# A graph network on one core: the last stage forms its self-connection on TensorE, normalizes on ScalarE, takes one power per block and stores from SyncE

## The reference

```python
xs = node_hiddens[:, :MUL]
xv = node_hiddens[:, MUL:].reshape(N, MUL, 3)
sc_s = xs @ wsc_s * inv                                  # the self-connection
sc_v = jnp.einsum('nud,uv->nvd', xv, wsc_v) * inv
ys = xs @ w1_s * inv
yv = jnp.einsum('nud,uv->nvd', xv, w1_v) * inv
...                                                      # messages over the edges, summed by node: ns, nv, deg
dn = jax.lax.rsqrt(jnp.maximum(deg, 1.0))
ns = ns * dn[:, None]
nv = nv * dn[:, None, None]
os_ = ns @ w2_s * inv2 + sc_s
ov = jnp.einsum('nud,uv->nvd', nv, w2_v) * inv2 + sc_v
os_ = os_ * jax.lax.rsqrt(jnp.mean(os_ * os_, axis=1, keepdims=True) + EPS) * g_s
rms_v = jax.lax.rsqrt(jnp.mean(ov * ov, axis=(1, 2))[:, None, None] + EPS)
ov = ov * rms_v * g_v[None, :, None]
# and around it
x = _layernorm(x + _L1_gnn_ref(x, ...), axis=-1)
```

## Time and profile before

| | us |
|---|---|
| median of 3 runs | 6196.12 (6193.98 to 6201.93) |
| the profiled execution | 6189.36 |
| its span in the trace | 6187.6 |
| TensorE busy | 5737.5 |
| VectorE busy | 5531.1 |
| GpSimd busy | 4743.6 |
| ScalarE busy | 3280.7 |

### The profile page before, as it was taken

One profiled execution on the slowest core, in us unless ns is written; L12 is line 12 of the kernel. 1 busy time (PEld: TensorE's weight loads), 2 busy tenths in 40 slices (PEclk: granted clock), 3 DMA queues, 4 the chain that ended last, 5 costly groups with the idle time before them and its releaser, 6 DMA issues.

```text
span 6187.6 us, 209904 instructions
## 1 busy us (share of the span) xinstructions
PE 5737.5 (93%) x40694; PEld 4573.5 (74%) x40695; DVE 5531.1 (89%) x17615; ACT 3280.7 (53%) x11999; POOL 4743.6 (77%) x4057
## 2 busy tenths in 40 slices
PE   6899999999999997889999999999999999999966
PEld 5555555555555554559999999999999999999944
DVE  2899999999999988989999999999999999999978
ACT  2566666666666654545555555555555555555522
POOL 2777777777777764548888888888888888888878
PEclk8999999999999998889999999999999999999999
DMA  6799999999999984459999999999999999999998
GB/s 198 222 264 263 263 263 263 263 263 264 264 264 263 264 253 152 157 147 178 178 178 178 175 177 176 176 175 175 177 174 177 175 176 174 177 176 174 167 298 294
DMA packets 1269400, 1298.01 MB, mean 210 GB/s; under 512 B 220911, under 2 KB 1180656, under 8 KB 1269264
## 3 DMA queue, kind: packets, MB, share of 16 engines
q0 software_dynamic: 328176, 468.28, 46.3%
q1 hardware_dynamic: 941186, 829.31, 45.6%
HBM read 695.20 MB, written 601.74 MB: 210 GB/s over the span
## 4 chain that ended last, share of the span: by engine, by line
PE 30%; DMA 14%; issue 9%; POOL 5%; DVE 2%; POOLq 1%; ACT 0%; SPq 0%; DVEq 0%; ACTq 0%
DMA part<-arena,c_idx 14%; PE PS L964 8%; PE PS L946 7%; PE PS L935 5%; PE PS L979 5%; PE PS L962 4%; POOL part L584 1%; POOL arena L565 1%; POOL arena L561 1%; POOL d_n L602 1%; POOL out L596 0%; PE PS L954 0%; DVE arena L1302 0%; ACT arena L753 0%; DVE arena L1299 0%
## 5 line engine op out<-in xcount | busy, mean ns | idle before, releaser
L584 POOL DMA_INDIRECT part<-arena,c_idx x1664 | 2615.1, 1572 | 538.3 <-issue 349.3
L545 POOL DMA_INDIRECT big<-h_tab,big x1664 | 1631.4, 980 | 511.7 <-issue 385.6
L860 PE MATMUL PS<-big 128*128 128x260 f32 x3328 | 953.2, 409 | 162.5 <-DVE big L1154 158.2
L964 PE MATMUL PS<-w2m,arena 128*128 128x128 f32 x6656 | 1103.8, 288 | 0.0
L946 PE MATMUL PS<-arena 128*128 128x256 f32 x3328 | 863.1, 382 | 27.9 <-ACT arena L753 26.7
L1162 DVE TENSOR_TENSOR big<-big,PS 128x260 f32 x1664 | 703.2, 423 | 207.9 <-PE PS L860 150.7
L964 PEld LDWEIGHTS PS<-w2m,arena 128*128 128x128 f32 x6656 | 876.9, 192 | 0.0
L860 PEld LDWEIGHTS PS<-big 128*128 128x128 f32 x3328 | 563.7, 189 | 422.6 <-issue 343.9
L659 ACT ACTIVATE big<-PS,arena 128x128 f32<-128x128 f32 x1664 | 513.6, 359 | 667.1 <-PE PS L850 667.1
L752 ACT COPY arena<-PS 128x512 f32<-128x512 f32 x832 | 488.7, 587 | 524.1 <-DMA part<-arena,c_idx 469.0
L729 ACT COPY arena<-PS 128x384 f32<-128x384 f32 x1664 | 718.6, 486 | 31.0 <-PE PS L935 2.8
(11 more groups left out here) (180 smaller groups left out, 10924.2 us busy)
## 6 DMA issues: line engine op xcount, KB each, us to landing
w_tab<-big SPq DMA_DIRECT2D x416, 520.0 KB
arena<-w_tab SPq DMA_DIRECT2D x1664, 130.0 KB
part<-arena SPq DMA_DIRECT2D x1664, 32.1 KB
ot_tab<-big SPq DMA_DIRECT2D x416, 128.0 KB
arena<-ot_tab SPq DMA_DIRECT2D x416, 128.0 KB
arena<-src_tab SPq DMA_DIRECT2D x416, 128.0 KB
arena<-part SPq DMA_DIRECT2D x392, 128.5 KB, 3.5
big<-h_tab,big POOLq DMA_INDIRECT x1664
```

Of the source, the lines that this page charges most:

```text
L545: pool.indirect_dma_start(hg[:, s, k, :], None, h_tab, bass.IndirectOffsetOnAxis(ap=sidx[:, s, k:k + 1], axis=0)).then_inc(s_hg[s], 16)
L584: pool.indirect_dma_start(part[q], bass.IndirectOffsetOnAxis(ap=c_idx[:, s, k:k + 1], axis=0), o_cmb[:, s, k, :], None, compute_op=ALU.add ...
L860: mm(PS[:, 2 + k % 2, 0:HW], oh[:, p, k, :], hg[:, p, k, :], start=True, stop=True).then_inc(s_agg, 1)
L964: last = mm(o_v[:, k, 2 * j:2 * j + 2, :].rearrange("p j u -> p (j u)"), midT[:, k, 1 + j, :], w2m[:, (1 + 2 * j) * MUL:(3 + 2 * j) * MUL] ...
```

## The change

In the node stage TensorE multiplies only by w1 (128 columns instead of 256), the copy L707 goes, and x1 alone is stored. In the final stage:

- TensorE transposes x1 of the block, ScalarE copies it from PSUM, TensorE multiplies it by `wsc`, ScalarE copies the result into `d_sc`, which takes the place of the loaded self-connection.
- VectorE packs degree, both mean squares and the variance, each of another block, into the four columns of `d_pk`; GpSimd takes one power of all four.
- The last normalization is ScalarE's: `d_z * rstd − mean * rstd`, with the bias `d_nm` formed by VectorE.
- SyncE issues the stores, six blocks behind. It loads x1 (256 columns instead of 512) together with the four tables, four blocks ahead, and waits for `s_do` of the block that held the buffer.
- The loop's body holds TURN_D = 8 blocks.

```diff
-    x1_tab = dram("x1_tab", [NP, 2 * D], F32)
+    x1_tab = dram("x1_tab", [NP, D], F32)
...
             def step_d(b, slot, there):                       # SyncE
+                s = slot % TURN
+                n, o = (slot + 4) % TURN_D, (s - 6) % TURN
                 if there(b + 4):
-                    wait(sp, s_dsum, b + 1)
+                    wait(sp, s_do, b + 1)
+                    sp.dma_start(d_x[:, n, :], one(x1b, b + 4)).then_inc(s_din[s], 16)
                     for k in range(GROUP):
                         sp.dma_start(d_p[:, s, k, :], one(pb[k], b + 4)).then_inc(s_din[s], 16)
-                n = (s + 2) % TURN
-                if there(b + 2):
-                    wait(sp, s_dz, b - 1)
-                    sp.dma_start(d_x[:, n, :], one(x1b, b + 2)).then_inc(s_dx[n], 16)
+                if there(b - 6):
+                    wait(sp, s_dout, b - 5)
+                    sp.dma_start(one(ob, b - 6), d_out[:, o, :]).then_inc(s_dst[o], 16)
...
             def step_d(b, slot, there):                       # GpSimd, all of it
+                wait_apart(pool, s_dout, b - 7)
+                wait(pool, s_dpk, b + 3)
+                g.tensor_tensor(d_pw[:, s, :], d_pk[:, s, :], half[:, :], ALU.pow).then_inc(s_dpw, 1)
...
             def step_d(b, slot, there):                       # ScalarE, behind the two squares
+                if there(b + 1):
+                    wait(act, s_dmap, b + 2)
+                    wait(act, s_do, b)
+                    a.copy(d_sc[:, (s + 1) % 2, :], PS[:, SC_BANK[(s + 1) % 2], 0:D]).then_inc(s_dsc, 1)
+                if there(b + 2):
+                    wait(act, s_dxp, b + 3)
+                    wait(act, s_dmap, b + 1)
+                    a.copy(d_xT[:, s % 2, :, :], PS[:, D_T_BANK, 0:2 * P].rearrange("p (k n) -> p k n", k=2)
+                           ).then_inc(s_dxT, 1)
+                if there(b - 5):
+                    wait(act, s_dnm, b - 4)
+                    wait(act, s_dst[o], landed(b - 9, o) if there(b - 9) else 0)
+                    scale, bias_col = d_pw[:, (s - 1) % TURN, VAR], d_nm[:, o, :]
+                    a.activation(d_out[:, o, 0:MUL], d_z[:, o, 0:MUL], ACT.Identity, bias=bias_col, scale=scale)
+                    a.activation(d_out[:, o, MUL:D].rearrange("p (u d) -> p d u", d=3),
+                                 d_z[:, o, MUL:D].rearrange("p (d u) -> p d u", d=3), ACT.Identity, bias=bias_col,
+                                 scale=scale).then_inc(s_dout, 1)
...
             def step_d(b, slot, there):                       # TensorE
+                if there(b + 2):
+                    wait(pe, s_din[(s + 2) % TURN], landed(b + 2, (s + 2) % TURN, 1 + GROUP))
+                    wait(pe, s_dxT, b + 2)
+                    for j in range(2):
+                        last = nc.tensor.transpose(PS[:, D_T_BANK, j * P:(j + 1) * P], d_x[:, x, j * P:(j + 1) * P],
+                                                   ident[:, :])
+                    last.then_inc(s_dxp, 1)
                 if there(b + 3):
...
+                if there(b + 2):
+                    wait(pe, s_dxT, b + 3)
+                    wait(pe, s_dsc, b + 1)
+                    for j in range(2):
+                        last = mm(PS[:, SC_BANK[s % 2], j * P:(j + 1) * P], d_xT[:, s % 2, j, :], wsc[:, j, :],
+                                  start=True, stop=True)
+                    last.then_inc(s_dmap, 1)
...
             def step_d(b, slot, there):                       # VectorE, in its new order
+                wait(dve, s_dpw, b - 1)
+                    v.tensor_scalar(d_pk[:, s, DEG], PS[:, TAB_BANK[n2], D:D + 1], 1.0, float(2 * MUL), ALU.max,
+                                    ALU.mult)
+                    v.tensor_scalar(d_pk[:, s, MS], d_sq[:, m1, :], EPS, None, ALU.add)
+                    v.tensor_scalar(d_pk[:, s, VAR], mv[:, s, 1:2], EPS, None, ALU.add).then_inc(s_dpk, 1)
...
+                    v.tensor_tensor(d_z[:, m3, :], d_z[:, m3, :], d_x[:, (slot - 3) % TURN_D, :], ALU.add).then_inc(s_dz, 1)
...
+                    v.scalar_tensor_tensor(d_o[:, n1, :], PS[:, TAB_BANK[n1], 0:D], d_pw[:, m1, DEG],
+                                           d_sc[:, (s + 1) % 2, :], ALU.mult, ALU.add).then_inc(s_do, 1)
```

More of the change, by code:

```diff
@@ L73, in landed, with steps @@
     return dmas * (16 // TURN * g + 16 - 16 // TURN * slot)
-def steps(eng, n, lead, tail, step):
-    first, last = 2 * TURN, (n - lead) // TURN * TURN
+def steps(eng, n, lead, tail, step, turn=TURN):
+    first, last = 2 * turn, (n - lead) // turn * turn
     for g in range(-lead, first):
[L82 to L85, removed]
+        step(g, g % turn, lambda v: 0 <= v < n)
+    with eng.Fori(first // turn, last // turn) as i:
+        for slot in range(turn):
+            step(i * turn + slot, slot, lambda v: True)
     for g in range(last, n + tail):
-        step(g, g % TURN, lambda v: 0 <= v < n)
+        step(g, g % turn, lambda v: 0 <= v < n)
 def bass_gat_equivariant_kernel(nc, x, xT, edges_sd, window_ends, ea8, ea4, W, WT, att_src, att_dst, bias, skip_W,
@@ L587, in _, with step_d @@
             steps(pool, NU, 0, 0, step_c)
[L590 to L603, removed]
-                    wait(pool, s_dmv, 3 * b)
-                    g.tensor_tensor(mv[:, m, 3:4], mv[:, m, 2:3], half[:, 0:1], ALU.pow).then_inc(s_drstd, 1)
-            steps(pool, NB, 2, 3, step_d)
+            def step_d(b, slot, there):
+                s = slot % TURN
+                wait_apart(pool, s_dout, b - 7)
+                wait(pool, s_dpk, b + 3)
+                g.tensor_tensor(d_pw[:, s, :], d_pk[:, s, :], half[:, :], ALU.pow).then_inc(s_dpw, 1)
+            steps(pool, NB, 2, 5, step_d, TURN_D)
         @block.scalar
@@ L768, in _, with step_d @@
-            steps(act, NB, 1, 0, step_d)
+            def step_d(b, slot, there):
+                s = slot % TURN
+                o = (s - 5) % TURN
+                if there(b):
+                    wait(act, s_do, b + 1)
+                    a.activation(d_q[:, 0:MUL], d_o[:, s, 0:MUL], ACT.Square, scale=float(1 / np.sqrt(MUL)),
+                                 accum_out=d_sq[:, s, 0:1])
+                    a.activation(d_q[:, MUL:D], d_o[:, s, MUL:D], ACT.Square, scale=float(1 / np.sqrt(3 * MUL)),
+                                 accum_out=d_sq[:, s, 1:2]).then_inc(s_dsq, 1)
+                if there(b + 1):
+                    wait(act, s_dmap, b + 2)
[14 more added lines that the diff above has]
+                                 scale=scale).then_inc(s_dout, 1)
@@ L771, in _ @@
+            steps(act, NB, 2, 5, step_d, TURN_D)
         @block.tensor
@@ L1390 @@
+                if there(b - 5):
+                    wait(dve, s_dpw, b + 2)
+                    v.scalar_tensor_tensor(d_nm[:, m1, :], mv[:, m1, 0:1], -1.0, d_pw[:, m1, VAR], ALU.mult, ALU.mult
+                                           ).then_inc(s_dnm, 1)
+                if there(b - 3):
+                    wait_apart(dve, s_dmv, 2 * (b - 3) + 1)
+                    v.bn_aggr(mv[:, m3, 0:2], stat[:, m3, :]).then_inc(s_dmv, 1)
+            steps(dve, NB, 2, 5, step_d, TURN_D)
 _WEIGHTS = ["bias", "skip_W", "w1_s", "w1_v", "wsc_s", "wsc_v", "w2_s", "w2_v", "fc_w1", "fc_w2", "fc_w3", "g_s", "g_v"]
```

147 lines of the change are left out of this document (70 added, 77 removed).

## The result

The changed kernel takes 6241.96 us (median of 4 runs, 6238.38 to 6248.27) against 6195.05 for the kernel before, run beside it: ratio 1.008, interval 1.0067 to 1.0094. It is slower, as forecast, but by 0.8% where 0.4% was forecast. The profiled execution's span is 6238.0 us against 6187.6, 50.4 longer.

| stage | before | after | difference | forecast |
|---|---|---|---|---|
| node stage | 2325.0 to 2749.3 | 2325.1 to 2740.1 | −9.2 | −11 |
| edge stage | to 5896.9 | to 5891.3 | +3.5 | 0 |
| final stage | to 6187.6 | to 6238.0 | +56.0 | +35 |

The account below looks back on a forecast made before the run. SyncE's issuing of six transfers was taken to bound the final stage. Final stage +35, node stage −11 and start +0.5 sum to +24.5: span 6187.6 becomes 6212, plus 8.5 over the span, forecast 6221 us; range 6194 to 6242.

Parts of the forecast that it names:

- Node stage, −11: Node stage: halved L907 and no copy L707 shorten VectorE's waits at low clock; −11 us (−14 to 0).
- SyncE 3.07 us a block: Final stage: SyncE issues six transfers instead of five and sets the block's time; 3.07 us (2.88 to 3.12).
- ScalarE 2.2 us, hidden under anything above that: Final stage: ScalarE's 0.70 us a block gains two copies (0.76) and two scaled passes (0.70), 2.2, hidden.
- the ring of load buffers: Final stage: load of b+4 waits for d_o(b); 10.3 us for four blocks, 2.6 each, below 3.07.
- The size: Final stage: 93 blocks give +31.6 us, the first d_o +3, the drain 0 (−2 to +3); stage +35.
- Rival D: Final stage: TensorE's three pieces each wait for ScalarE; 3.3 us a block or more, 6241 us or more; chance 0.08.
- Rival A: Final stage: SyncE not the limit; buffer reuse (2.6 us) or TensorE (2.5 to 2.8) is; 6176 us; chance 0.11.
- B: Final stage: SyncE's address arithmetic is hidden; 2.88 us a block, stage +17, 6203 us; chance 0.16.
- C: Node stage: clock falls, +25 us instead of −11, 6257 us; sign, a mean clock below 0.8; chance 0.05.
- GpSimd's power of four columns: Final stage: one power of four columns takes GpSimd 0.73 to 1.1 us a block, far from any bound.
- TensorE, "2.5 to 2.8": Final stage: with two transposes and two matmuls added, TensorE takes 2.5 to 2.8 us a block, at most 3.0.
- DMA engines 2.34 us: Final stage: a block moves 770 KB instead of 898, so 2.73 us scaled with the bytes becomes 2.34.

Follow-up runs that it names:

- either opening of the ring: Changed kernel with either ScalarE's copy d_sc moved ahead of the squares (ratio 1.0042) or VectorE's d_nm moved ahead of the x1 addition (1.0041).
- the store alone: Kernel before with only the output store moved from GpSimd to SyncE; ratio 1.0052, final stage 328.2 us.
- the last version: Changed kernel with d_sc copied before the squares, d_nm moved earlier, two-block transfers, part loads six blocks ahead, stores eight behind; ratio 0.9955 to the kernel before.
- d_nm early: Changed kernel with VectorE's d_nm moved ahead of the addition of x1 in its step; 6226.56 us beside 6198.04 for the kernel before, ratio 1.0041.
- the paired kernel four ahead: Changed kernel with d_sc copied before the squares, d_nm moved earlier, SyncE's transfers for two blocks at a time, four blocks ahead; ratio 1.001 to the kernel before.

## Why the prediction was right and wrong

- **Node stage, −11: right in this profile.** Measured −9.2. Over the ten profiles with the new node stage it is −7 on average, from −13 to +2 (see the last section). VectorE waits 3.8 us for L707 (old L706), forecast under 6, 16.3 in the earlier trace rows. From the waits of the kernel after, 2325 to 2740 us:

```profile
DVE arena L1315 <- ACT big L707: 3.8, 7, 0.8
```

- **SyncE 3.07 us a block: nearly right as a price, wrong as the bound.** 3.14 in the changed kernel, 3.12 to 3.15 with either opening of the ring, and 3.14 to 3.18 on the kernel before with the store alone; each is at or just above the forecast's upper 3.12.
- **"ScalarE 2.2 us, hidden under anything above that": the step that failed.** The 2.2 was nearly right (143.01/71.5 = 2.00 us a block), and so was VectorE's 2.2 (149.56/71.5 = 2.09). What failed is the word hidden. A sum of busy times hides an engine only where its work may slide. ScalarE's order did not let it: an instruction that waits for the end of VectorE's step stood ahead of one that VectorE's next step waits for. The forecast went through the ring of load buffers, but not through this one, though all of its members were in its own terms: output passes 0.82, squares 0.57, copy 0.44, and VectorE from d_o to d_nm 1.24 with 0.28 of handover. Sum 3.35, and it is above 3.07. The two passes were priced at 0.70 and cost 0.82; without that the circle would still be 3.2.
- **The size.** 97 distances of 3.314 instead of 2.716 us: +58.0 (forecast +31.6). The first d_o comes 12.3 us after the stage's start instead of 9.2: +3.1 (forecast +3). From the last d_o to the end 12.9 instead of 18.0: −5.1 (forecast 0, at best −2), since SyncE's last store ends the span 7.4 us sooner than GpSimd's. Together +56.0. So the ring cost 26 us more than the forecast's block, and 5 us of that were hidden by an end that it had not counted.
- **Rival D** had the size, 3.3 us a block and 6241 us (measured 6241.96), but other partners: TensorE's pieces waiting for ScalarE. TensorE's waits here are for part loads (48.4 us). Its time fit for the wrong reason, and with 0.08 it was held too low: a ring through ScalarE's queue should have been the second case.
- **Rival A** (SyncE not the limit) is what the last version shows, at 2.44 us a block and not 2.6; it took half of the transfers, a longer lead and the open ring. **B**: the address arithmetic is not hidden, 0.56 to 0.61 for the store. **C** did not come, though the clock fell: 0.80 instead of 0.86, with TensorE at 322 of 415 us. Its sign, a mean clock below 0.8, came in seven of the ten new profiles, and even at 0.76 the stage took 425 us, 1 to 2 more than with the old one and not 25.
- **GpSimd's power of four columns**, 0.73 to 1.1: 1.16, just above. It costs nothing here: GpSimd waits for VectorE before it (157.8 of 240 us). TensorE, "2.5 to 2.8": 191.46/71.5 = 2.68.
- **DMA engines 2.34 us:** a share of 0.81 of 3.355 is 2.72; in the last paired version it is 2.44 us at 1.01. Scaling the share with the bytes was too simple: 235 GB/s at 0.81 would be 290 at full share, but 320 GB/s at 1.01 is 317 and 338 at 1.02 is 331.

The Trainium skill's page "DMA: Bandwidth & Descriptors", section "Issuing engines are not separate DMA queues", calls the time to start a transfer usually small beside the transfer. For one transfer the trace agrees, and the prediction set it against the page too readily: 0.47 us of issue beside 3.5 us to landing. But the starts add up on one engine, while landings overlap: the store alone on SyncE cost 0.47 us a block, +37.5 us in the stage. With the ring closed, on the other hand, the store's place changed nothing in the loop, which is the outcome that the prediction drew from the rule, for another reason.

## What to carry to other kernels

Before calling an engine hidden, write down for each of its instructions what it waits for and who waits for it, and follow the circle through the queues of two engines by the distances of starts; if it is longer than the fullest engine's work, it is the block's time, as it was here. In an in-order queue, the instruction that waits for the latest event goes last, and the one that another engine waits for goes first: here each such move alone took some 19 us off the stage at no work. Then look at the engine that starts transfers: its price is mostly per transfer, so fewer and larger ones can pay. They beat the kernel before only when they were started far enough ahead and with the ring open; pairing the part loads of the kernel before cost 25 to 30 us.

## What the runs showed of the hardware

- **Starting a transfer costs SyncE by the piece.** Four of 128.5 KB take 1.77 us in the kernel with d_nm early, four of 257 KB 1.94 in the paired kernel four ahead, and 2.10 in the one six ahead, with the DMA engines full: 0.04 to 0.08 us more each for twice the bytes.
- **The span ends later behind a store of GpSimd than behind one of SyncE.** From the start of the last store's issue to the end of the span it is 9.6 us in all six profiles in which GpSimd issues it, and 2.1 to 2.5 us in all eight in which SyncE does, though both land about 2 us after their issue. On GpSimd a drain instruction fills the rest (to 0.2 us before the end in the kernel before).
- **The granted clock of the node stage was lower with less TensorE work.** With the old node stage (TensorE busy 342 to 344 of 423 us) its mean was 0.86 to 0.87 each time and the stage took 423 to 424 us. With the new one (L907 at half its columns) it was 0.76 to 0.81, and the stage took 411 to 425 us, the longest at 0.76 and the shortest at 0.80 to 0.81; mean of ten 417. So the saving of 9.2 us is 7 on average. That the lower clock gives part of it back fits these numbers, but was not tested, and why the clock lies anywhere from 0.76 to 0.81 with the same work stays open. Busy times of 415 us of this stage, first the kernel after:

```profile
2325.00:2740.00 415.00, 321.92 (x1176) 195.72 (x1176) 383.77 (x1078) 179.76 (x490) 215.10 (x294) 0.80 0.42 124
```

and the kernel with d_nm early, whose stage starts 3 us later:

```profile
2325.00:2740.00 415.00, 326.81 (x1151) 197.62 (x1151) 374.40 (x1047) 173.81 (x474) 211.87 (x291) 0.77 0.41 124
```

  At 0.77 TensorE is busy for longer (327 us) with fewer matmuls (1151). The Trainium skill's page "TensorE: Matmul & The Clock Gate", section "What's actually happening", has the clock follow how busy TensorE has been; the lower mean after the change agrees with that, the spread at equal work is not told by it.
- **Chips differ by 11% on the same program.** From 500 to 1500 us, in the first stage, the changed kernel gets through 779 gathers on one chip and 580 on the other, by the groups of that stretch. On the one:

```profile
L558 POOL DMA_INDIRECT big<-h_tab,big x779 | 763.0, 979 | 237.6 <-PE PS L878 116.5 <-issue 63.7 <-ACT big L652 57.4
```

On the other (the kernel after, run again):

```profile
L558 POOL DMA_INDIRECT big<-h_tab,big x580 | 572.8, 988 | 428.1 <-PE PS L878 233.9 <-issue 131.6 <-remote 60.9
```

  A gather's issue takes the same there (979 and 988 ns); it is the waiting between them that grew, at 196 GB/s instead of 263 and a granted clock of 0.93 instead of 1.00. What makes that chip slower there is open. The final stage of the changed kernel ran alike on both (346.8 and 345.2 us).
